# The comparison loop of an attention kernel: quotients on GpSimd, VectorE's inverses two batches behind, another place for one spread of q

## The reference

```python
Z = jnp.concatenate([k_proj, q_proj], axis=1).transpose(0, 2, 1)
idx = jnp.argsort(Z, axis=2)
...
context = jnp.take_along_axis(context_s, inv[..., None], axis=2)[:, :, T:]
...
norm_sorted = 2.0 * sum_relu - (Z_sort * total_v - total_vz)
...
norm = jnp.maximum(norm, 0.0001)
context = 2.0 * context / norm[..., None]
```

## Time and profile before

| | us |
|---|---|
| median of three runs | 1204.36 (1202.58 to 1205.13) |
| the profiled execution, its time | 1203.41 |
| its span | 1201.6 |
| the comparison loop, first masks to last statistics | 132.7 to 304.1 |

### The profile page before, as it was taken

One profiled execution on the slowest core, in us unless ns is written; L12 is line 12 of the kernel. 1 busy time (PEld: TensorE's weight loads), 2 busy tenths in 40 slices (PEclk: granted clock), 3 DMA queues, 4 the chain that ended last, 5 costly groups with the idle time before them and its releaser, 6 DMA issues. The chain is left out here.

```text
span 1201.6 us, 20133 instructions
## 1 busy us (share of the span) xinstructions
PE 873.4 (73%) x5730; PEld 700.2 (58%) x5732; DVE 778.2 (65%) x2421; ACT 658.0 (55%) x1352; POOL 513.9 (43%) x634
## 2 busy tenths in 40 slices
PE   3796666666238999986995366777668989999910
PEld 2633455554227888975993133444456979999900
DVE  5479589898775457112676799998868641115636
ACT  4355777776544225653664676676775645555500
POOL 0002555554226666667774773000005663035155
PEclk9998678787557999997997688798877999999965
DMA  7960000000601116645763110000031133223132
GB/s 205 289 184 1 1 0 0 0 0 1 249 13 43 47 61 192 200 136 154 198 171 95 46 46 25 1 1 1 1 137 49 45 112 91 64 82 90 41 97 61
DMA packets 133844, 97.01 MB, mean 81 GB/s; under 512 B 11648, under 2 KB 125696, under 8 KB 132736
## 3 DMA queue, kind: packets, MB, share of 16 engines
q1 hardware_dynamic: 121472, 70.79, 19.7%
q0 software_dynamic: 12288, 25.19, 7.2%
HBM read 45.61 MB, written 50.33 MB: 80 GB/s over the span
## 5 line engine op out<-in xcount | busy, mean ns | idle before, releaser
L1125 POOL DMA_INDIRECT e_xs<-h_tok,rows_of x128 | 128.6, 1005 | 104.0 <-DVEq L1618 35.4
L739 ACT ACTIVATE mask<-ps_q,k_neg 128x256 bf16<-128x256 f32 x256 | 100.7, 488 | 35.0 <-PE ps_q L853 35.0
L1138 POOL DMA_INDIRECT e_got<-e_ys,e_rows_of x64 | 66.2, 1035 | 115.7 <-DMA e_ys<-e_y_rows 87.5
L1781 DVE TENSOR_TENSOR e_hidden<-e_ps_gu,e_hidden 128x512 f32<-128x512 f32 x48 | 33.2, 691 | 97.1 <-ACT e_hidden L1464 97.0
L853 PE MATMUL ps_q<-q_parts,pick 128*128 (+1 forms) x256 | 56.6, 360 | 51.9 <-DVE mask L651 46.3
L1274 PE MATMUL e_ps_gu<-e_w_all,e_x_turned 128*128 x384 | 91.9, 383 | 0.3 <-ACT e_x_turned L1457 0.3
L1469 ACT ACTIVATE e_hidden<-e_ps_up 128x512 f32<-128x512 f32 x80 | 47.8, 597 | 73.4 <-PE e_ps_up L1312 73.2
L1125 POOL DMA_INDIRECT e_xs<-h_tok,e_rows_of x64 | 66.1, 1033 | 49.8 <-DVEq L1618 19.8
L1329 PE MATMUL e_ps_y<-e_w_all,e_h_turned 128*128 x640 | 84.3, 275 | 0.0
L2286 POOL DMA_INDIRECT c_got<-e_ys,rows_of x64 | 71.3, 1114 | 30.0 <-issue 19.2
L651 DVE TENSOR_TENSOR mask<-ps_q,k_tok 128x1024 bf16<-128x1024 f32 x64 | 75.2, 1216 | 10.2 <-PE ps_q L853 8.2
(11 more groups left out here) (411 smaller groups left out, 2601.5 us busy)
## 6 DMA issues: line engine op xcount, KB each, us to landing
e_x_rows<-e_xs SPq DMA_DIRECT2D x68, 256.0 KB, 2.8
e_ys<-e_y_rows SPq DMA_DIRECT2D x68, 256.0 KB, 2.4
e_xs<-zeros SPq DMA_DIRECT2D x2, 6144.0 KB, 34.2
e_w_all<-in_w SPq DMA_DIRECT2D x4, 1536.0 KB, 13.4
e_xs<-zeros SPq DMA_DIRECT2D x2, 2560.0 KB, 27.4
e_w_all<-in_w SPq DMA_DIRECT2D x4, 1024.0 KB, 10.9
x_tok<-in_x SPq DMA_DIRECT2D x4, 512.0 KB, 6.1
e_xs<-h_tok,rows_of POOLq DMA_INDIRECT x128, 2.3
```

Source lines behind the costliest of these rows:

```text
L739: last = nc.scalar.activation(mask[u][QS // 2 + j][keys][:, h * T:(h + 1) * T], psq[1][:, h * T:(h + 1) * T], ACT.Sign, bias=k_neg[u][:, k ...
L1125: nc.gpsimd.indirect_dma_start(out=xs[part], out_offset=bass.IndirectOffsetOnAxis(ap=rows_of[:, t * K + k:t * K + k + 1], axis=0), in_=til ...
L1138: nc.gpsimd.indirect_dma_start(out=got[t % GB][:, k * P:(k + 1) * P], out_offset=None, in_=ys[part], in_offset=bass.IndirectOffsetOnAxis(a ...
```

## The change

Six things change, all in this block.

1. The quotient moves from VectorE (L682) to GpSimd (`quotients`). In GpSimd's step b, `quotients(b - 2)` stands first, ahead of the columns of batch b, and waits for a new semaphore `inverse_out`.
2. The numerators take 9 columns per head in place of 8, so the unweighted norm comes out of GpSimd's two instructions, and VectorE's first two small instructions (L674, L675) go. The columns of a head are laid out as v, weight, k * v, k times the weight.
3. GpSimd's third part of tile 2b + 1 now stands ahead of `numerators(b - 1)`, which was ahead of it.
4. VectorE's step b is now: masks of quad 0; row statistics of b - 3; inverses of b - 2 (subtract, max, reciprocal); masks of quad 1; sums of b - 1.
5. TensorE spreads quad 1 right ahead of quad 2, between the products of quads 0, 1 and those of quads 2, 3.
6. `pipelined_from` puts the first 4 steps (VectorE) or 2 (GpSimd) ahead of the loop; two steps and the last row statistics come behind it.

```diff
+def pipelined_from(eng, n, first, step):
+
+    assert n % 2 == 0 and first % 2 == 0
+    for i in range(first):
+        step(i, i % 2)
+    with eng.Fori(0, (n - first) // 2) as i2:
+        step(i2 * 2 + first, 0)
+        step(i2 * 2 + first + 1, 1)
...
-            num = tb("num", T)
+            num = tb("num", TPB * HEADS * (HD + 1))
...
-                    def results(b_):
-                        c = Chain(dve, batch_self, b_ * steps)
-                        dve.wait_ge(sums_out, FROM + b_ + 1)
-                        S = sums[:, :].rearrange("p (h r) -> p h r", r=VC)
-                        q = at(q_tok, b_ * (TPB * HEADS), TPB * HEADS)
-                        num3 = num[:, :].rearrange("p (h r) -> p h r", r=HD)
-                        c.link(nc.vector.tensor_tensor(n1[:, :], S[:, :, 2 * HD], q, ALU.mult))
-                        c.link(nc.vector.tensor_tensor(n1[:, :], n1[:, :], S[:, :, 2 * HD + 1], ALU.subtract))
-                        c.link(nc.vector.tensor_tensor(n1[:, :], n1[:, :],
-                                                       at(half_counts, b_ * (TPB * HEADS), TPB * HEADS), ALU.subtract))
-                        c.link(nc.vector.tensor_scalar(n1[:, :], n1[:, :], 0.5e-4, None, ALU.max))
-                        c.link(nc.vector.reciprocal(n1[:, :], n1[:, :]))
-                        assert c.n == steps, c.n
-                        dve.wait_ge(num_out, FROM + b_ + 1)
-                        nc.vector.tensor_tensor(at(y_tok, b_ * T, T).rearrange("p (h r) -> p h r", r=HD), num3,
-                                                n1[:, :].unsqueeze(2).broadcast_to([P, TPB * HEADS, HD]),
-                                                ALU.mult).then_inc(y_made, 1)
+                    def row_sums(b_):
                         dve.wait_ge(y_made, FROM + b_ + 1)
                         for t in range(TPB):
                             nc.vector.bn_stats(at(stats, b_ * (TPB * 6) + t * 6, 6),
                                                at(y_tok, b_ * T + t * P)).then_inc(stats_done, 1)
 
+                    def inverses(b_):
+                        c = Chain(dve, batch_self, b_ * steps)
+                        num3 = num[:, :].rearrange("p (h r) -> p h r", r=HD + 1)
+                        dve.wait_ge(num_out, FROM + b_ + 1)
+                        c.link(nc.vector.tensor_tensor(n1[:, :], num3[:, :, HD],
+                                                       at(half_counts, b_ * (TPB * HEADS), TPB * HEADS), ALU.subtract))
+                        c.link(nc.vector.tensor_scalar(n1[:, :], n1[:, :], 0.5e-4, None, ALU.max))
+                        nc.vector.reciprocal(n1[:, :], n1[:, :]).then_inc(inverse_out, 1)
+                        assert c.n == steps, c.n
+
                     def step(b_, parity):
-                        now, before = not is_at(b_, NB), not is_at(b_, 0)
+                        now = not is_at(b_, NB) and not is_at(b_, NB + 1)
                         if now:
                             masks(b_, parity, 0)
-                        if before:
-                            sums_in(b_ - 1)
+                        if not is_at(b_, 0) and not is_at(b_, 1):
+                            if not is_at(b_, 2):
+                                row_sums(b_ - 3)
+                            inverses(b_ - 2)
                         if now:
                             masks(b_, parity, 1)
-                        if before:
-                            results(b_ - 1)
-                        else:
+                        if is_at(b_, 0):
                             constant_parts()
-                    pipelined(dve, NB, step)
+                        elif not is_at(b_, NB + 1):
+                            sums_in(b_ - 1)
+                    pipelined_from(dve, NB, 4, step)
+                    step(NB, 0)
+                    step(NB + 1, 1)
+                    row_sums(NB - 1)
...
-                    nc.gpsimd.tensor_copy(c3[:, :, 2 * HD], head_weight[:, :])
+                    nc.gpsimd.tensor_copy(c3[:, :, HD], head_weight[:, :])
...
-                        nc.gpsimd.tensor_tensor(c3[:, :, HD:2 * HD], v3,
+                        nc.gpsimd.tensor_tensor(c3[:, :, HD + 1:2 * HD + 1], v3,
...
+                    def quotients(b_):
+                        pool.wait_ge(inverse_out, FROM + b_ + 1)
+                        nc.gpsimd.tensor_tensor(
+                            at(y_tok, b_ * T, T).rearrange("p (h r) -> p h r", r=HD),
+                            num[:, :].rearrange("p (h r) -> p h r", r=HD + 1)[:, :, 0:HD],
+                            n1[:, :].unsqueeze(2).broadcast_to([P, TPB * HEADS, HD]),
+                            ALU.mult).then_inc(y_made, 1)
+
                     def numerators(b_):
+                        pool.wait_ge(y_made, FROM + b_)
                         pool.wait_ge(sums_out, FROM + b_ + 1)
                         S = sums[:, :].rearrange("p (h r) -> p h r", r=VC)
-                        num3 = num[:, :].rearrange("p (h r) -> p h r", r=HD)
-                        q_b = at(q_tok, b_ * (TPB * HEADS), TPB * HEADS).unsqueeze(2).broadcast_to([P, TPB * HEADS, HD])
-                        nc.gpsimd.tensor_tensor(num3, S[:, :, 0:HD], q_b, ALU.mult).then_inc(num_own, 1)
+                        num3 = num[:, :].rearrange("p (h r) -> p h r", r=HD + 1)
+                        q_b = at(q_tok, b_ * (TPB * HEADS), TPB * HEADS).unsqueeze(2).broadcast_to(
+                            [P, TPB * HEADS, HD + 1])
+                        nc.gpsimd.tensor_tensor(num3, S[:, :, 0:HD + 1], q_b, ALU.mult).then_inc(num_own, 1)
                         pool.wait_ge(num_own, FROM + b_ + 1)
-                        nc.gpsimd.tensor_tensor(num3, num3, S[:, :, HD:2 * HD], ALU.subtract).then_inc(num_out, 1)
+                        nc.gpsimd.tensor_tensor(num3, num3, S[:, :, HD + 1:VC], ALU.subtract).then_inc(num_out, 1)
 
                     def step(b_, parity):
                         now, before = not is_at(b_, NB), not is_at(b_, 0)
+                        if before and not is_at(b_, 1):
+                            quotients(b_ - 2)
                         if now:
                             pool.wait_ge(qk_sb, FROM + AHEAD + b_ + 1)
                             parts = [vals[parity][:, j * HEADS * HV:(j + 1) * HEADS * HV].rearrange(
@@ -812,11 +833,12 @@
                             third_part(b_ * TPB, parts[0])
                             columns(b_ * TPB + 1)
                             remainder(b_ * TPB + 1, parts[1])
+                            third_part(b_ * TPB + 1, parts[1]).then_inc(vals_ready, 1)
                         if before:
                             numerators(b_ - 1)
-                        if now:
-                            third_part(b_ * TPB + 1, parts[1]).then_inc(vals_ready, 1)
-                    pipelined(pool, NB, step)
+                    pipelined_from(pool, NB, 2, step)
+                    step(NB, 0)
+                    quotients(NB - 1)
...
                             mask_values(b_ - 1, 1 - parity, 1)
                         if now:
+                            spread_q(b_, 1)
                             spread_q(b_, 2)
                         if before:
                             mask_values(b_ - 1, 1 - parity, 2)
                             mask_values(b_ - 1, 1 - parity, 3)
                         if now:
-                            spread_q(b_, 1)
                             spread_q(b_, 3)
                     pipelined(pe, NB, step)
 
```

More of the change, by code:

```diff
@@ L600, in attention0 @@
             sums = tb("sums", TPB * HEADS * VC)
-            num = tb("num", T)
+            num = tb("num", TPB * HEADS * (HD + 1))
             n1, half_counts = tb("n1", TPB * HEADS), tb("half_counts", TILES * HEADS)
-            num_out, num_own, y_made = map(sem, ("num_out", "num_own", "y_made"))
+            num_out, num_own, inverse_out, y_made = map(sem, ("num_out", "num_own", "inverse_out", "y_made"))
             self_done = sem("dve_done")
@@ L607, in attention0 @@
             ksum_ps, ksum_sb = sem("ksum_ps"), sem("ksum_sb")
-            cols_self, cols_ready, hi_ready, mid_ready, rest_ready = map(
-                sem, ("cols_self", "cols_ready", "hi_ready", "mid_ready", "rest_ready"))
+            cols_ready, hi_ready, mid_ready, rest_ready = map(
+                sem, ("cols_ready", "hi_ready", "mid_ready", "rest_ready"))
             vals_ready = sem("vals_ready")
@@ L634, in _ @@
                                                     at(rs, b_, 1), ALU.subtract, ALU.mult).then_inc(qk_rows, 1)
-                    steps = 5
+                    steps = 2
                     def constant_parts():
```

## The result

The changed kernel takes 1223.5 us (median of 4 runs, 1221.56 to 1226.33); the kernel before, beside it, 1203.47. The ratio is 1.0168, with a 95% interval of 1.015 to 1.0186. It is slower by 20 us.

What follows compares the result with a forecast made beforehand. The prediction took ScalarE's timeline as the pace, 10.24 us a batch, with VectorE nearly full. Start 3.5, loop 17.6 and tail 0.9 sum to 22.0 us on 1203.41, 1225.4; it said 1225.5, range 1216 to 1232.

Steps and rivals of the forecast that it cites:

- The ring: Loop from X(b), start of batch b's quad-3 signs, through GpSimd, VectorE, ScalarE to X(b+1): 11.29 to 11.77 us against 10.24.
- The clock's share: In the loop's spread of quad 3, TensorE's two clock levels share evenly: 11.5 us a batch, costing 17.6 us.
- The start: Before the loop, spread 1 waits for VectorE's first masks and delays ScalarE's first signs: 3.5 us more.
- The tail: After the loop, everything from the last product to the last statistic runs in series: 0.9 us more.
- behind the block: Later phases start behind a barrier and move as a block, with no change of their own.
- VectorE's loss: VectorE in the loop sheds L674, L675, L682: 1.68 us a batch, busy time down some 25 us.
- What I called covered: In the loop, VectorE's remaining work, about 8.5 us, and the earlier spread of quad 1 cost nothing.
- Rival 1: Loop: VectorE stays the bound and the moved work is hidden; 8.56 us a batch, 1184 us, faster; chance 0.05.
- Rival 2: Loop: only the quotient's order matters, chain passes through VectorE's masks; 10.41 us a batch, 1210 us; chance 0.07.
- Rival 3: Loop: the chain plus contention between GpSimd and VectorE, 0.34 us more a batch, 1230 us; chance 0.1.
- Rival 4: Loop: the wait only moves, 10.24 us a batch stays, the change does little; 1208 us; chance 0.01.
- The rule that spoke the other way: Loop: optimize the most occupied engine first, so work taken off VectorE, at 87%, should pay.

Runs made afterwards that it cites:

- experiment 1: Changed kernel with GpSimd's quotient of b-2 moved from ahead of the columns of tile 2b to behind that tile's remainder; 1207.06 us, ratio 1.003.
- experiment 2: Changed kernel with GpSimd's numerators of b-1 back ahead of the third part, quotient still ahead of the columns; 1209.76 us, ratio 1.0059.
- experiment 7: Changed kernel with the quotient back on VectorE, right behind the reciprocal, all else as changed; ratio 1.0073 to the kernel before.
- experiment 9: Changed kernel with one more GpSimd product of the quotient's size, unread, ahead of the quotient and behind the wait for inverse_out; 1232.23 us, ratio 1.0249.
- Experiment 3: Changed kernel with TensorE's spread of quad 1 back at the end of the step, behind the products of quads 2 and 3; 1223.54 us, ratio 1.0168.
- experiment 5: Kernel before with only TensorE's spread of quad 1 moved ahead of that of quad 2; ratio 1.054 on a chip where before took 1330.0 us.
- Experiment 4: Changed kernel with the quotient behind the columns, as in experiment 1, and TensorE's spread of quad 2 ahead of quad 1's; 1194.96 us, ratio 0.9939.

## Why the prediction was right

**The ring.** Forecast from X(b): 1.97 third part, 2.61, 4.19, reciprocal done 5.09, quotient done 5.91, signs 7.11, their end 10.46, X(b+1) at 11.29 or 11.77. In the batch shown: 1.97, 2.63, 4.19, 5.14, 5.90 (the columns' start), 7.12, 10.46, 11.77; in nine of the fourteen batches it is 11.28 to 11.31, so the sum stands link by link. Experiments 1, 2, 7 and 9 show it as a ring and not only as a sum: opened at either of its two new links it gives back 14 to 15.5 us of the loop, lengthened by 0.59 it costs 0.59.

**The clock's share.** I took the middle between the two levels, 11.5; but only four of the 14 batches were longer than the 11.3 of the upper level (11.77, 11.47, 11.46, 11.38), and one was shorter, 11.17. The mean was 11.35. This term was 2.1 us too high. The middle came from the mean clock of the whole loop, and from two spreads of which the slow one stood behind a long idle time. Neither settles the level of this one spread. These rows hold it together with the next spread 0:

```profile
219.57 2.08 PE L875 MATMUL ps_q<-q_parts,pick 128*128 x8 [2.47 <-ACT mask L748]
...
288.17 1.22 PE L875 MATMUL ps_q<-q_parts,pick 128*128 x8 [2.63 <-ACT mask L748]
```

The same eight matmuls took 1.22 behind 2.63 us of idleness and 2.08 behind 2.47. The first stands in a batch of 11.77, the second in one of 11.29.

**The start.** Forecast 3.5, measured 4.75. X(0) came 0.5 later than said (142.20 against 141.7), and X(1) followed 10.51 later, not 9.8. I had taken the middle for the two spreads ahead of its signs, and they ran at the lower level (2.05, to the signs 2.15, where I had 1.65), as in the batch of experiment 1 shown. The products took 1.44, where my sum leaves about 1.1 for them and the row that I named only says at most 1.65. Experiment 3 confirms where the cost comes from. **The tail** cost 0.2 in place of 0.9: the last products ended at X+7.0 (318.60), not X+7.37, and from there to the last statistic it was 5.96, not 6.25. The three errors come to 1.5 us too much, and the 0.4 behind the block, which I had at nothing, leaves 1.1 in 22. That the errors have different signs is luck; the median of the runs lies 2.0 under the 1225.5 that I said.

**VectorE's loss.** I expected its busy time down by some 25 us; it is 16.9. The 1.68 us a batch were measured from start to start and hold idle gaps. The instructions removed (L674, L675, L682) were busy for 20.0 us of the stretch, 1.43 a batch, in part at the same time as their neighbours. It made no difference to the sum, as VectorE has room.

**What I called covered.** The place of spread 1 was said to cost nothing in the loop, with the old place as good. Experiment 3 says it is better than that: the old one would have cost 0.38 us a batch. TensorE was through both spreads at X+6.2 in the batch shown, not X+5.3, still ahead of the signs. And I hadn't seen that the change's parts need each other (experiment 5).

**The rivals.** Rival 1 (faster) fell: its condition, a wait for the inverse that ends before X+3.35, was not met; it ends at X+5.3. Experiment 4 shows what may be right in it: once the columns don't wait and spread 2 goes first, the changed kernel's parts are worth 7 to 8 us against the kernel before. How much of that is VectorE's freed time and how much its new order, no run separates: experiment 4 with the quotient on VectorE wasn't run. No run came near its 1184; the fastest median beside a kernel before of 1203 is 1193.75. Rival 2's ring exists, and experiment 2 runs at it. Rival 3 (contention) fell: the quotient took 0.626 to 0.635 us in all 16 batches, the row of L800; the Trainium skill's rule (SBUF — State Buffer, Who interferes with whom), by which a VectorE instruction with two SBUF inputs contends with GpSimd's reads and one with a single SBUF input doesn't, agrees with this, as VectorE's masks, which ran beside it, read one operand from PSUM. VectorE's own quotient did contend with GpSimd, as the last section shows. Rival 4 fell: the ratio is 1.0168.

**The rule that spoke the other way**, to optimize the engine of the highest occupancy first (the Trainium skill, Perfetto Trace Analysis, Identifying the Most-Contended Engine): the traces don't bear it out in this change, where VectorE went from 129.41 to 112.50 us and the stretch from 143.42 to 158.92. In experiment 4 VectorE is busy for 110.62 us and the stretch is 134.20, which agrees with it, but other orders changed there too. It goes by the busy shares, and here the order in the queues decided.

## What to carry to other kernels

When work moves between engines that take instructions in order, don't only ask whether the new engine has room: write down what stands behind each new wait in its queue, follow it until it comes back to the engine that ends the wait, and add up that ring. Here it was 11.3 us against a pace of 10.24, with GpSimd idle for 43% of it; with the same instruction further back, behind the columns, the pace was 10.30. Test such a ring by lengthening one link by a known amount, and try an edit's parts alone before keeping one of them: each may be there for another.

## What was not expected of the hardware

- TensorE's granted clock doesn't follow from its work alone: for the same 1176 matmuls between X(1) and X(15) it was 0.77 before, 0.69 in the changed kernel, 0.59 in experiment 5 and 0.79 to 0.82 in the two fastest. The total idle time doesn't give it either: in experiment 2 the stretch is as long as before (143.38 and 143.42 us) and TensorE was idle for longer (53.0 against 48.3 us), at 0.82 against 0.77. What does is open.
- Where VectorE's quotient met GpSimd's remainder (L789 of the kernel before), the one that began second was slowed. In the kernel before the quotient began 0.05 to 0.06 us behind it in 13 of 16 batches and took 0.96 or 0.97; once it began 0.34 behind it and took 0.68; twice no GpSimd operation ran beside it, and it took 0.42 and 0.43. In experiment 7 it began first and took 0.42, and in 12 batches the remainder, 0.16 to 0.18 behind it, took 0.85 to 0.87 in place of 0.74. Each time the second one lost some 0.14 us less than the time from its start to the first one's end.

```profile
193.83 0.74 POOL L789 TENSOR_TENSOR rest<-cols,vals 128x288 f32<-128x288 f32 x1 [0.55 <-ACT vals L746]
193.88 0.97 DVE L682 TENSOR_TENSOR y_tok<-num,n 128x256 f32 x1
```

```profile
208.38 0.42 DVE L693 TENSOR_TENSOR y_tok<-num,n 128x256 f32 x1
208.55 0.85 POOL L802 TENSOR_TENSOR rest<-cols,vals 128x288 f32<-128x288 f32 x1 [0.55 <-ACT vals L759]
```

- On one chip the part behind the block took 1018 to 1031 us in four traces, and 895 to 899 in the nine others, with the comparison loop at the same pace. What differs there wasn't looked into.
